# Two attention layers on one core: scores on 32-row tiles, four heads at a time

## What is computed

```
layer 0: logits = q k^T / sqrt(8) - softplus(alpha_h) * |i - j|;  softmax;  times v;  times out_w;  + out_b
         ffn: tanh(x W1 W2 W3 + bias)
layer 1: q = x W_q; k, v from (x W_k + x W_v) W_down W_up;  scores = q k^T / sqrt(128) * exp(-0.01 |i - j|);  softmax
         ffn: 128 -> 512 -> 512 -> 128 with weights of +1 and -1, relu between them
```

## Time and profile before

| | us |
|---|---|
| median of three runs | 417.1 |
| the profiled execution | 419.92 |
| its span, first to last instruction | 418.1 |
| PE / DVE / ACT / POOL busy | 365.7 / 348.1 / 305.6 / 132.7 |
| first scores reach DVE | 36.88 |
| first copy of a finished attention (`acc_sb`, item 0) | 66.72 |
| the same of item 7 | 204.77 |
| the same of item 15 | 386.97 |

### The profile page before, as it was taken

How to read it: one execution, slowest core, us unless ns; L and a number is a source line. 1 busy time by engine, 2 the same in 40 slices (tenths; PEclk the granted TensorE clock), 3 DMA queues, 4 the chain that set the end, 5 groups by cost and what they waited for, 6 DMA issues and landing times.

```text
span 418.1 us, 10844 instructions
## 1 busy us (share of the span) xinstructions
PE 365.7 (87%) x3493; PEld 284.6 (68%) x3493; DVE 348.1 (83%) x1618; ACT 305.6 (73%) x661; POOL 132.7 (32%) x302
## 2 busy tenths in 40 slices
PE   2125989999999999999989898999999999999755
PEld 1014767777778787787767676768778877786643
DVE  5335899999999999999999999899998979894431
ACT  3212878878888888788877787888788788788442
POOL 5042333242433334332313142343524323331100
PEclk9999999999999999999999999999999999999866
DMA  2352522222222222213121212112221200000000
GB/s 64 95 117 64 133 51 53 52 53 52 53 52 51 59 56 61 71 45 73 39 65 38 67 38 58 26 48 53 52 63 48 66 8 14 2 16 2 13 14 13
DMA packets 28006, 20.82 MB, mean 50 GB/s; under 512 B 4199, under 2 KB 26926, under 8 KB 26926
## 3 DMA queue, kind: packets, MB, share of 16 engines
q1 hardware_dynamic: 27374, 19.87, 19.3%
q10 hardware_dynamic: 576, 0.26, 0.3%
HBM read 10.68 MB, written 9.44 MB: 48 GB/s over the span
## 4 chain that ended last, share of the span: by engine, by line
PE 64%; DVE 19%; ACT 7%; issue 6%; POOL 2%; ACTq 1%; DVEq 0%; POOLq 0%
PE bank L404 17%; PE bank L382 11%; PE bank L416 10%; PE bank L442 8%; DVE scored L637 7%; DVE scored L648 5%; PE bank L424 3%; PE bank L461 3%; PE bank L453 3%; PE bank L401 3%; ACT fr L781 2%; PE bank L521 2%; ACT fh L779 2%; PE bank L393 1%; DVE adist L1160 1%
## 5 line engine op out<-in xcount | busy, mean ns | idle before, releaser
L788 ACT ACTIVATE probs<-bank 128x512 f32<-128x512 f32 x256 | 151.9, 599 | 52.0 <-PE bank L404 34.5
L404 PE MATMUL bank<-ident,scored 128*128 128x128 f32 x896 | 135.6, 273 | 1.0 <-ACT scored L796 1.0
L648 DVE TENSOR_SCALAR scored<-scored,mx 128x256 f32<-128x256 f32 x320 | 110.9, 388 | 0.0
L404 PEld LDWEIGHTS bank<-ident,scored 128*128 128x128 f32 x896 | 105.1, 140 | 6.1 <-ACT scored L796 2.7
L637 DVE CUSTOM_DVE_ANT_0 scored<-bank,adist 128x256 f32<-128x256 f32 x256 | 96.6, 418 | 12.0 <-PE bank L382 11.0
L637 DVE CUSTOM_DVE_ANT_0 scored<-bank,decay 128x256 f32<-128x256 f32 x256 | 96.7, 417 | 11.8 <-PE bank L382 11.2
L382 PE MATMUL bank<-stack 96*128 96x256 f16 x512 | 99.8, 277 | 3.7 <-DVE mx L637 3.4
L382 PEld LDWEIGHTS bank<-stack 96*128 96x128 f16 x512 | 44.0, 99 | 37.0 <-DVE mx L637 19.3
L416 PE MATMUL bank<-probs,vpad 128*32 128x256 f32 x1024 | 68.5, 385 | 0.0
L796 ACT ACTIVATE scored<-scored,negbias 128x256 f32<-128x256 f32 x128 | 58.0, 508 | 0.0
L958 POOL TENSOR_SCALAR negbias<-mx 128x2 f32<-128x2 f32 x64 | 16.2, 252 | 130.6 <-DVE mx L637 130.6
(11 more groups left out here) (145 smaller groups left out, 449.9 us busy)
## 6 DMA issues: line engine op xcount, KB each, us to landing
stack<-dqk SPq DMA_DIRECT2D x32, 256.0 KB, 3.9
dqk<-parts SPq DMA_DIRECT2D x124, 64.0 KB, 2.1
out_dram<-outb SPq DMA_DIRECT2D x8, 128.0 KB, 1.8
x_sb<-in_L_attn_x_dram SPq DMA_DIRECT2D x1, 640.0 KB, 6.1
x_sb<-in_L_attn_x_dram SPq DMA_DIRECT2D x1, 256.0 KB, 3.1
dqk<-parts ACTq DMA_DIRECT2D x4, 64.0 KB, 2.1
bool_raw<-in_L_ffn_k_dram SPq DMA_DIRECT2D x1, 256.0 KB, 3.6
w_raw<-in_L_attn_qkv_w_dram SPq DMA_DIRECT2D x1, 192.0 KB
```

Source lines behind the costliest of these rows:

```text
L404: mm = pe.transpose(dst, src, ident[:, :])
L648: sh = dve.tensor_scalar(scored[:, r, t, :], scored[:, r, t, :], mx[:, 2 * r + t:2 * r + t + 1], None, ALU.subtract)
L788: act.activation(probs[:, c % RING, :, :], turn_bank(c)[:, :].rearrange("p (a c) -> p a c", a=2), ACT.Exp).then_inc(probs_ready, 1)
```

## The change

Scores are computed for four heads at once. `stack` now holds four heads below one another, 32 rows each, and `pe_scores` issues eight matmuls per group of four heads, each on its own 32-row tile of the array and into its own bank, 0 to 3. It does so in slots 1, 5, 9 and 13, ahead of the product with v in the same slot, and only when DVE has finished the last maximum of the group before. `dve_max` moves one slot later. `TURN_BANKS` goes from three banks to two. All other work of PE borrows banks 0 and 1 of the scores, or bank 7. The weights of q and k are permuted so that the channels of a tile stand together; the number of bytes over DRAM stays. `SHIFT` goes from 8 D, 4 A, 4 P per item in layer 0 to 5 D, 5 A, 6 P, and from 12 D, 4 A in layer 1 to 11 D, 4 A, 1 P, in other places. In the head the zeroing of `stack` goes, item 0's q and k go separately through smaller steps, ACT issues the loads of the weights, and the preparation of item 2 moves into iteration 0. In the tail the order of the last two items' steps is new, and DVE does the last norm.

```diff
-PART_ROWS = 2 * HD
-K_SCORE = 96
+PAD = 96
+QUAD = 4
 RING = 8
 LAG = 4
-TURN_BANKS = (2, 3, 4)
-ACC_BANK = 5
...
+TURN_BANKS = (4, 5)
+ACC_BANK = 6
+MISC = 7
...
-    "qk": (2, 2), "v": (3, 3), "xn": (14, 14), "stats0": (2, 2), "stats1": (3, 3), "mean": (4, 4), "norm": (10, 10),
...
+    "qk": (2, 2), "v": (3, 3), "xn": (14, 15), "stats0": (2, 2), "stats1": (3, 3), "mean": (4, 4), "norm": (10, 10),
...
+FIRST = {"qk": 9, "hi": 11, "low": 11, "stats0": 6, "stats1": 7, "mean": 8, "norm": 11}
...
-SHIFT = ("DPDADPDADPDADPDA", "DDADDDADDDADDDAD")
+SHIFT = ("APDP" "APDA" "APDP" "ADPD", "ADDD" "ADDD" "ADDD" "ADDP")
...
+    def pe_scores(pe, it, g):
+
+        par, first = it % 2, H * it + QUAD * g
+        if it == 0:
+            if g % 2 == 0:
+                pe.wait_ge(ld_first[g // 2], 32)
+        elif g == 0:
+            pe.wait_ge(ld_stack[par], stack_loads(it))
+        need(pe, max_ready, first)
+        bank_free(pe, 0)
+        bank_free(pe, 1)
         for t in range(QT):
-            mm = pe.matmul(ps_score[s % 2][:, t * T:(t + 1) * T], stack[0:K_SCORE, par, 0, h, t * P:(t + 1) * P],
-                           stack[0:K_SCORE, par, 1, h, :], start=True, stop=True)
-        mm.then_inc(score_ps, 1)
+            for j in range(QUAD):
+                rows = slice(32 * j, 32 * j + 32)
+                mm = pe.matmul(bank[j][:, t * T:(t + 1) * T], stack[rows, par, 0, g, t * P:(t + 1) * P],
+                               stack[rows, par, 1, g, :], start=True, stop=True, tile_position=(32 * j, 0))
+                if t == QT - 1:
+                    mm.then_inc(score_ps, 1)
+        for j in range(2):
+            last_reader[j] = (max_ready, first + j + 1)
...
-            pe_scores(pe, c)
+            if s % QUAD == 1:
+                pe_scores(pe, i, s // QUAD)
+                if c >= 9:
+                    g = (c - 9) // 4
+                    pe_pv(pe, g // 4, g % 4)
             if c >= LAG:
                 pe_turn(pe, c - LAG)
-            if s % 4 == 1 and c >= 9:
-                g = (c - 9) // 4
-                pe_pv(pe, g // 4, g % 4)
...
+            if i == 0 and s == 6:
+                pe_xn_t(pe, 2)
...
-            dve_max(dve, c)
-            if c > 0 and shift_of(c - 1) == "D":
-                dve_shift(dve, c - 1)
+            if c >= 1:
+                dve_max(dve, c - 1)
+            if c >= 2 and shift_of(c - 2) == "D":
...
         pe_turn(pe, HEADS - 1)
-        pe_hidden(pe, a, 3, [0, 1])
+        pe_hidden(pe, a, 3, [0])
         pe_pv(pe, c, 3)
+        pe_hidden(pe, a, 3, [1])
+        pe_acc_t(pe, c)
         pe_hidden(pe, b, 0, [0, 1])
-        pe_acc_t(pe, c)
         pe_hidden(pe, b, 1, [0, 1])
         pe_att_t(pe, c)
+        pe_proj(pe, c)
         pe_out(pe, a)
-        pe_proj(pe, c)
         pe_hidden(pe, b, 2, [0, 1])
+        pe_ft(pe, c)
         pe_hidden(pe, b, 3, [0, 1])
-        pe_ft(pe, c)
-        pe_out(pe, b)
         pe_hidden(pe, c, 0, [0, 1])
         pe_hidden(pe, c, 1, [0, 1])
+        pe_out(pe, b)
...
+        dve.tensor_copy(acc_sb[:, T:2 * T], ps_acc[:, T:2 * T]).then_inc(acc_half, 1)
+        for step in range(3):
+            dve_attention(dve, c, step)
         low_hidden(dve, a, 3)
         low_hidden(dve, b, 0)
-        for step in range(3):
-            dve_attention(dve, c, step)
-        low_hidden(dve, b, 1)
         dve_residual(dve, c)
         dve_f_stats(dve, c, range(QT))
         dve_f_mean(dve, c)
+        dve.wait_ge(f_stats, 4 * (c + 1))
+        dve.tensor_scalar(fvpe[:, 0:QT], fmv[:, :, 1], EPS, None, ALU.add).then_inc(f_rstd, 1)
+        low_hidden(dve, b, 1)
+        dve.wait_ge(f_rstd, 3 * (c + 1))
+        dve.wait_ge(ft_ps, c)
+        for t in range(QT):
+            norm = dve.tensor_scalar(fxn[:, t, :], x_item(c)[:, t, :], fmv[:, t, 0:1], frstd[:, t:t + 1], ALU.subtract,
+                                     ALU.mult)
+        norm.then_inc(f_xn, 1)
...
+    def bounce(eng, n, w, p):
+
+        for copy in range(2):
+            row = 2 * p + copy if w else 2 * copy + p
+            eng.dma_start(dqk[n % 2][w, :, row, :, :], parts[:, p, w, :]).then_inc(bounced, 16)
 
...
+        if n == 0:
+            for half in range(2):
+                for w in range(2):
+                    sp.dma_start(stack[:, 0, w, 2 * half:2 * half + 2, :],
+                                 dqk[0][w].rearrange("a b g t -> (a b) g t")[:, 2 * half:2 * half + 2, :]
+                                 ).then_inc(ld_first[half], 16)
+            return
...
-        clear(dve, 0, 0)
-        clear(dve, 0, 1)
...
+        dve.wait_ge(wk_ps, 1)
+        for r in range(2):
+            cp = dve.tensor_copy(by_tile(w0_t[:, 1, :])[:, r], by_row(bank[5][:, 0:D])[:, r])
+        cp.then_inc(wk_sb, 1)
+        dve.wait_ge(ln_rstd, 3)
+        for t in range(QT):
+            norm = dve.tensor_scalar(xn[:, t, :], x_sb[:, t, :], mv[:, t, 0:1], rstd[:, t:t + 1], ALU.subtract, ALU.mult)
+        norm.then_inc(ln_xn, 1)
...
+        dve.wait_ge(q0_ps, 1)
+        dve.tensor_scalar(xf[:, 0, :], bank[7][:, 0:T], bias0_cols[:, 0:1], SCALE[0], ALU.add, ALU.mult).then_inc(q0_sb, 1)
+        dve.wait_ge(q0_sb, 1)
+        dve.tensor_copy(parts[:, 0, 0, :], xf[:, 0, :]).then_inc(q0_hi, 1)
+        dve.wait_ge(q0_hi, 1)
+        dve.tensor_tensor(parts[:, 1, 0, :], xf[:, 0, :], parts[:, 0, 0, :], ALU.subtract).then_inc(q0_lo, 1)
+        dve.wait_ge(k0_sb, 2)
+        dve.tensor_tensor(parts[:, 1, 1, :], xf[:, 1, :], parts[:, 0, 1, :], ALU.subtract).then_inc(lo_ready, 1)
         dve.wait_ge(iota_ready, 1)
...
+        for n, h in enumerate(ORDER):
+            dve.tensor_scalar(adist[:, h, :], toe_abs[:, :], al_tmp[:, 1, h:h + 1], None,
+                              ALU.mult).then_inc(adist_ready, 1)
+            if n == 11:
+                dve_hi(dve, 1)
+        dve.wait_ge(adist_ready, H)
...
+        act.wait_ge(k0_ps, 1)
+        act.activation(xf[:, 1, :], bank[6][:, 0:T], ACT.Identity, bias=bias0_cols[:, 1:2]).then_inc(k0_sb, 1)
+        act.activation(parts[:, 0, 1, :], bank[6][:, 0:T], ACT.Identity, bias=bias0_cols[:, 1:2]).then_inc(k0_sb, 1)
+        act.wait_ge(k0_sb, 2)
+        bounce(act, 0, 1, 0)
+        act.wait_ge(lo_ready, 1)
+        bounce(act, 0, 1, 1)
+        act.activation(al_warm[:, :], al_tmp[:, 2, :], ACT.Exp)
+        act.wait_ge(wv_ps, 1)
...
-        act_norm_attention(act, 2)
-        act_xn(act, 2)
```

303 lines of the change are left out of this document (182 added, 121 removed), and 4 rows, old and new, of the table SLOTS.

## The result

| | before | after |
|---|---|---|
| median of four runs, us | 417.5 | 446.8 |
| lowest to highest | 416.64 to 420.33 | 444.14 to 449.19 |
| ratio | | 1.069 [1.061, 1.077] |
| span of the profiled execution | 418.1 | 445.2 |
| first maximum | 36.88 | 22.50 |

A forecast was written before the change was run, and what follows sets the result against it. PE was taken to bound layer 0, DVE the first items of layer 1. Layer 0 +7.5, layer 1 -8, head -15.5 and tail -4.5 summed to -20.5 us, a median of 397; range 375 to 409.

The forecast's parts named there:

- Head and tail: Before the first maximum and after the last items: -15.5 us from an earlier first maximum, -4.5 from an earlier h2.
- no cost: Iteration 0: taking on item 2's preparation adds a few tenths on engines not yet full, counted as nothing.
- Part 1, the scores: Scores on PE: a group of four heads costs 0.34 us with the change of tile shape, saving 2.16 per item.
- two rounds: Scores on PE: eight matmuls per group run as two rounds of four row tiles at 0.11, 0.22 us.
- tiles one after another: Rival, scores on PE: row tiles do not overlap, adding 42 us, total 439, slower; chance 0.04.
- slow weight loads: Half of a rival, scores on PE: each round needs 0.22 for weight loads, total 411; chance 0.20 shared with a weaker head.
- Part 2: Shifts and two turn banks, layer 0: waits for ACT add 2.8 us per item, making it 20.8; +7.5 in all.
- three chains on ACT: Layer 0, exponentials and shifts before the turns of heads 8, 12 and 4: PE waits 1.61, 0.78 and 0.38 us.
- head 0 waits for nothing: Layer 0: the q, k and v projections stand between, so head 0's A shift adds no wait.
- Part 3: Layer 1: items with both halves of the ffn take 23.4 us against 24.70; -8 us in all.
- The same waits are smaller: Layer 1: ffn pieces stand between the turns, so heads 8 and 0 keep about 1.5 us of waits together.
- PE's 21.9: Layer 1: PE's own work per item falls from 23.85 us busy to 21.9.

The follow-up runs named there:

- b_turn2: The kernel before with two turn banks instead of three, nothing else: 417.9 us, 1.003.
- b_item2: The kernel before with item 2's layer norm and transposes moved from the head into iteration 0, and item 3's preparation to later slots: 422.1 us, 1.013.
- a_noA: The changed kernel with every A shift turned into P: 410.9 us, 0.983 of the kernel before.
- a_best_head2: a_pvafter_A3_v6_att with item 2's layer norm and transposes put back in the head: 413.3 us, 0.988 of the kernel before.
- a_v6: The changed kernel with the v projection and its copies moved from slot 3 to 6: 442.4 us, 1.059 of the kernel before.
- a_pvafter_A3_v6_att: The best kernel: the changed one with product behind the first turn, A at each group's last head, v, att and proj in later slots: 409.3 us, 0.981.
- b_pair: The kernel before with scores issued for two heads at once, in the even slots: 423.4 us, 1.011.
- the table: Changed kernel, A as changed, at last heads, or none: product with v ahead of the turns 446.8, 439.2, 410.9 us; behind the first 440.4, 413.8, 412.4.

## Why the prediction was wrong

**The steps that failed, in short.** The prediction had ACT late only at single places, ahead of the turns of four A heads, and on time everywhere else. That put 2.8 us per item on it in layer 0 and 1.5 in layer 1, and no wait of PE's scores for ACT at all. The waits that it walked in layer 0 came as walked. But the shifts make ACT late through the item, the scores wait for its copies out of their banks, and layer 1 kept nothing of what PE saved: +42.9 us in the two layers for -0.5.

**Head and tail were right, the tail in part by luck.** -14.4 for -15.5, and -6.2 for -4.5, of which 1.1 was to come ahead of `acc_sb`. The tail's product `h2` starts 15.4 after `acc_sb` of item 15 where it was 18.4, so the reordering gave 3.0, for 3.4. Another 2.9 is that `h2` now takes 3.68 instead of 6.56, at full clock, and that is not the change's doing: in `b_turn2` and `b_item2`, which have the old tail, it takes 3.68 too. The profiled execution of the kernel before had the lower clock there, 0.55.

**Iteration 0, "no cost", was +4.8.** `a_noA` has 2.5 less there, so that much goes with the A shifts; the move of item 2 is 1.5 by `a_best_head2`. The rest, 0.8, wasn't split. In the changed kernel the granted clock is 0.95 in this stage and 1.00 in `a_noA`; at most 0.05 x 34.6 = 1.7 of the 2.5 are that (an estimate).

**Part 1, the scores, was right.** Row tiles run at once: of the eight matmuls at 126.16 the first four start within 0.01 us, the second four 0.12 later, as the forecast's two rounds. The chain's piece is 0.33 for eight, change of shape included, for 0.34 forecast; 0.40 behind a wait. The first heads of kind P behind the product show 0.33 where the earlier trace rows has 0.22. The rival of tiles one after another is out, and so is that of slow weight loads, 0.12 for eight. By the 3.07 of the Trainium skill, "TensorE: Matmul & The Clock Gate", Part 3, an estimate, they would take 0.29 and with the change of shape 0.40; the trace has 0.33, so the tiles do better here than that figure.

**Part 2 had the mechanism and failed in its sum.** Its three chains on ACT were right. From the start of turn 5 to that of turn 8 it had 3.34, from turn 9 to turn 12 2.54, and from turn 1 to turn 4 as much; the trace has 3.36, 2.57 and 2.57.
But an item came to 22.60, not 20.8. The prediction walked a few places with ACT on time at the start of each. ACT is not: its queue is in order and it is late from one group into the next, until PE's scores wait for it as well. At 141.90 PE starts the two transposes of `fxn`, 0.22; the scores behind them start at 143.53, 1.4 late, because ACT's copies of v are not out of bank 1. That wait is most of the missing 1.8 per item and was named nowhere in the forecast, although the diff put v into a bank of the scores. That head 0 waits for nothing was true of its turn and missed its shift, which is on the chain at 140.18, ahead of those copies. The rest is small pieces, such as 0.2 ahead of `fxn` and ahead of one product with v. `a_v6` shows that the wait at v is a sign of the lateness and not its cause: it went and 0.4 came back.

**Part 3 is where it failed most**: 23.4 per item was forecast and 25.98 to 28.62 came. Two terms were wrong, and the runs part them.
- *The A shifts.* "The same waits are smaller" put 1.5 per item on them, 0.6 net of the four additions that P would need in their place; `a_noA` is 15.8 us shorter over eight items, 2.0 each. Some of that is the clock, 0.97 against 1.00: at most 0.03 x 205 = 6 us (an estimate). Again the waits for the shifts themselves were smaller than forecast, 6.8 us or 0.85 per item, and those of the scores for ACT's copies, which had no term, larger: 9.2 and 5.7, or 1.9 per item. The ffn's pieces between the turns were counted as cover for PE, but ACT has the ffn's relus to do in the same time; that this is why was argued, not tested.
- *The bound behind PE.* The sum took PE's 21.9 as if PE stayed the bound. DVE was busy 45.02 of 49.41 there, 22.5 per item, so 2.2 was the most that a faster PE could give with DVE's work as it was, or 2.9 with the D shift (0.67) that it loses, and only if DVE never idled. The forecast of -1.3 lies inside that; but DVE does idle more: it waits 17.2 us for scores in layer 1 of `a_noA`, 11.2 in the kernel before. Without any A, layer 1 takes 189.1, still 6.9 over the kernel before, and the best kernel's items take 25.0 to 25.5 where 23.2 to 24.7 stood. `b_pair` shows that issue in groups costs something here: 2.4 us for pairs. What groups of four cost by themselves was not run.

**The cause, in one sentence:** the change takes the product with v, the only long piece that covered a shift on ACT, from between the turns, and puts the A heads where nothing else covers them. Shown by the table: 33 of the 447 us go when both are undone, and 36 when the shifts leave ACT. How the loss reaches PE differs by place: waits of the turns for a shift, and waits of the scores for copies that stand behind the shifts in ACT's queue. Of the rivals none was it. Row tiles one after another, 439, was the nearest in number and is excluded by the trace; the chance of 0.04 for slower went to it, and none of its own to the forecast's chain running longer than walked. The sign turned there: the two layers were to give 0.5 us between them and cost 43.

Left open: how much of layer 1's loss is the lower granted clock (0.96 and 0.97 in the windows above, 1.00 before) beyond the bound above, how far issue in groups of four is the reason that the two layers of the best kernel together are slower than before, and why the clock stays low so much longer in iteration 0 of `b_item2` (0.50 to 0.64 over 12 us) than in the other kernels.

## What to carry to other kernels

When an in-order engine hands a result back to the one that bounds the kernel, look for the piece of work that hides the round trip, and count a reordering by whether that piece still lies between; walk at least two periods, with the helper starting late. When the bounding engine gets faster by x, the gain is at most its distance to the next engine, and issue in groups can take from that, because both must then meet once a group with nothing in reserve. A new order and a new assignment can each look harmless or bad alone: run the two by two.

## What the runs showed of the hardware

- Four 32-row tiles run at once (126.16 us of the kernel after: starts within 0.01 us, the second round 0.12 later): eight matmuls of 32 rows and 256 columns in f16 take 0.33 us in a stream, their eight weight loads 0.12. Timeline of PE's weight loads, one group:

```profile
126.16 0.12 PEld L432 LDWEIGHTS bank<-stack 32*128 32x128 f16 x8 [0.17 <-issue]
```

- A change of tile shape costs the piece behind it 0.10 to 0.11 us: 0.33 for 0.22 at the P matmuls behind the product, as 0.32 for 0.22 at the scores behind it before.
- A turn that starts behind a wait holds the next piece back by 0.05 us beyond the wait: 0.49 from start to start instead of 0.44. A chain of waits, read from end to end, shows it as 0.66 instead of 0.44, because the 0.16 that in a stream lies under the next piece is then in the open.
- A move of work can change the clock: in `b_item2` the granted clock went to 0.50 after PE was busy 2.64 of 4 us, and a move that brought the start 4.4 us forward had the first `acc_sb` 4.3 behind. The same move in `a_pvafter_A3_v6_att` stayed at 1.00, with PE busy only 2.23 of 4 us in one window, so busy time alone does not tell the two apart.
